# Two layers of an audio tower: the first feed-forward's residual in two VectorE steps, its second-norm statistics kept for all sequences, VectorE's loop written out

## The chip, the cores and the metric

The kernel runs on one core of a Trainium2 chip. The metric is the device time of one execution in microseconds (us), median of the runs. Engines are called PE (TensorE, matrix products), DVE (VectorE), ACT (ScalarE), POOL (GpSimd) and SP (which issues DMAs). Each engine takes its instructions in program order and waits on semaphores for the others.

## What is computed

Sixteen sequences of 256 tokens and 192 features pass a token selection (179 of 256 kept), and then two layers of attention and feed-forward, each ahead of a layer norm and with a residual. The part that the change touches is the second half of the first layer and the norm behind it:

```python
def _fq(x, scale, qmin, qmax):
    q = jnp.clip(jnp.round(x / scale), qmin, qmax) * scale
    return x + jax.lax.stop_gradient(q - x)
...
h = jnp.einsum('bsd,hd->bsh', x, _quant_weight(W1)) + b1
h = jax.nn.gelu(h, approximate=False)
h = _fq(h, s_gelu, -128.0, 127.0)
y = jnp.einsum('bsh,dh->bsd', h, _quant_weight(W2)) + b2
y = _fq(y, s_out, -128.0, 127.0)
...
h = h + _L0_ffn_ref(_layernorm(h, axis=-1), ...)
h = h + _L1_attn_ref(_layernorm(h, axis=-1), ...)
```

The second attention begins with a fake quantization whose scale is the largest absolute value of the whole normed tensor, over all 16 sequences. So nothing of the second attention can start before the last sequence has left the feed-forward and its norm.

## The kernel before

The residual stream of all sequences lies in SBUF (`resid`, 128 partitions, two token tiles of 128 and 51 rows per sequence). The program is written engine by engine, with semaphores; its stages follow one another. The change lies in the stage between the two attentions, the feed-forward of layer 0, which runs as a software pipeline over the 16 sequences (`ffn_step(i, par)` on PE, ACT and DVE).

- **PE**, step i: `ffn_turn(i)` transposes the normed sequence i + 1, `ffn_hidden(i)` makes the 768 hidden features of sequence i (24 f32 matmuls, L1909 and L1910), `ffn_out(i)` multiplies the quantized hidden features of sequence i - 1 with W2 (12 bf16 matmuls, L2078). `ffn_out(b)` waits for `hq_ready` (the quantized features from DVE) and for `f_added` of sequence b - 1, which frees its PSUM bank.
- **ACT**, step i: copies the transposed tile out of PSUM (L983), six Gelus (L994), one conversion to int32 (L1000), which sets `gelu_done`.
- **DVE**, step i, in this order: `ffn_norm` normalizes sequence i + 2 for the first norm (L1409); `ffn_add` takes y of sequence i - 2 out of PSUM and adds it to the residual in four dependent instructions, scale and bias (L1449), clip (L1453), round by adding and subtracting a large number (L1455), times `s_out` plus residual (L1458), through an f32 buffer `y_sb`; `hidden_round` clips the hidden features of sequence i - 1 to bf16 (L1465); `norm_max(i - 5)` normalizes sequence i - 5 for the second norm (L1488) and takes its largest absolute value (`top_abs`, L1497); `pair_tile_stats` takes mean and variance statistics of the newest residual (L1471, `bn_stats`).
- **POOL** first clears buffers for the next stages (memsets, L766 to L782), and then turns the statistics of two sequences at a time into mean and reciprocal standard deviation (`pair_norms`, L801 to L822: 20 links, each a tiny 128x4 instruction that waits for the one before). It waits for `pair_stats` ahead of them, and, ahead of L812, for `norm_used`.

The statistics and results for a pair stand in single buffers (`tstats`, `tmean`, `trstd`, four columns each). That is why POOL must wait at L812 until DVE has used the pair before, and DVE waits for `stats_taken` before it writes new statistics. DVE's steps 0 to 5 are written out, 6 to 13 are a hardware loop of two steps (`staged`), and the end is written by hand: the last two sequences get their statistics by DVE itself (`last_stats`, `last_pair`), and sequences 12 and 13 are normalized by POOL (L830).

When 14 sequences have their maximum, PE starts eight dummy products (`warm_up(8)`, L2041). Behind them it transposes the column of maxima (L2276, waits for `x_maxed`), then runs `warm_up(9)`, and then transposes the first quantized sequence for the second attention. DVE takes the overall maximum (L1567, then L1569 from PSUM) and quantizes (L1580 to L1586).

## Time and profile before

| | us |
|---|---|
| median of three runs (1355.39 to 1357.83) | 1355.62 |
| span of the profiled execution, first to last instruction | 1353.8 |
| outside the span, median less span | 1.8 |
| DVE, stage of the feed-forward: first `ffn_add` to the overall maximum | 842.7 to 941.5 |
| busy in the span: PE / DVE / ACT / POOL | 1116.0 / 1102.3 / 987.6 / 868.5 |

Times inside the profile are microseconds from the start of the span. In the timeline a row is one or more consecutive instructions of a kind: start, duration, engine, line, operation, output<-input and the count; the bracket tells how long the engine sat idle before it and what released it. POOLq stands for POOL's sequencer (a semaphore step without arithmetic). A row's duration overlaps the next row's start by the pipeline's length, so the cost of an instruction in a chain is the distance from start to start. In the table of windows each engine has its busy time with the number of instructions; PEclk is the granted clock of PE as a share of 2.4 GHz.

### The profile page before, as it was taken

To read this page: it belongs to the slowest core of one execution; us is meant where nothing else is said; L and a number is where in the kernel's file an instruction comes from. 1 tells how busy PE (TensorE), PEld (TensorE's weight loads), DVE (VectorE), ACT (ScalarE), POOL (GpSimd) and SP (SyncE) were. 2 spreads that over 40 slices of the span, in tenths; PEclk is the share of its full clock that TensorE was granted. 3 is DMA by queue.
4 is the path that set the end of the run, shared out by engine and by line. 5 is a ranking of instruction groups with operands and counts; after the bars stand their busy time and mean duration, and the time that the engine had idled before them with its cause. 6 is when DMAs were issued, how large, how long until landed. Compare 5 with 4: busy or idle time off the path is not lost. (4 is left out here: it accounts for less than half of the span.)

```text
span 1353.8 us, 40911 instructions
## 1 busy us (share of the span) xinstructions
PE 1116.0 (82%) x17093; PEld 855.6 (63%) x17093; DVE 1102.3 (81%) x2146; ACT 987.6 (73%) x921; POOL 868.5 (64%) x954
## 2 busy tenths in 40 slices
PE   3766877888787778788887877985999999998796
PEld 2454655666565556556665656883677777776595
DVE  7879989899999999999999994877567777777343
ACT  0469999999999999999999995772434444443232
POOL 4079889898889888988898897744011322324254
PEclk9889999999999999999999999997999999999698
DMA  9999999300000000000000001100000200002351
GB/s 251 360 361 359 355 339 335 102 11 11 10 8 5 11 10 2 10 11 10 2 11 10 11 2 48 24 0 0 2 2 2 65 19 18 16 12 56 108 153 56
DMA packets 78532, 107.61 MB, mean 79 GB/s; under 512 B 6963, under 2 KB 76489, under 8 KB 78356
## 3 DMA queue, kind: packets, MB, share of 16 engines
q1 hardware_dynamic: 66138, 90.93, 20.6%
q0 software_dynamic: 5360, 8.02, 1.8%
q10 hardware_dynamic: 6860, 6.12, 1.8%
q8 instruction: 135, 2.21, 0.7%
q14 instruction: 39, 0.32, 0.1%
HBM read 18.32 MB, written 83.85 MB: 75 GB/s over the span
## 5 line engine op out<-in xcount | busy, mean ns | idle before, releaser
L968 ACT ACTIVATE work<-work 128x2864 f32<-128x2864 f32 (+1 forms) x272 | 704.8, 2704 | 15.7 <-DVE work L446 14.8
L446 POOL TENSOR_TENSOR work<-shared 128x1253 f32<-128x1253 f32 (+1 forms) x272 | 613.1, 2268 | 114.3 <-PE psum L1956 78.8
L1956 PE MATMUL psum<-work,ws_place 128*32 128x179 f32 x8640 | 397.5, 322 | 148.6 <-ACT work L968 137.6
L446 DVE TENSOR_TENSOR work<-psum,shared 128x1611 f32<-128x1611 f32 (+3 forms) x288 | 488.0, 1723 | 0.5
L1956 PEld LDWEIGHTS psum<-work,ws_place 128*32 128x32 f32 x8640 | 264.3, 111 | 248.9 <-ACT work L968 191.4
L2154 PE MATMUL psum<-shared 32*64 32x179 f32 (+1 forms) x1728 | 129.4, 341 | 1.3 <-DVE peaks L1606 1.0
L957 ACT ACTIVATE pt_region<-psum,bs_neg 128x384 f32<-128x384 f32 x144 | 100.2, 697 | 2.9 <-PE psum L1968 2.9
L2154 PEld LDWEIGHTS psum<-shared 32*64 32x64 f32 (+1 forms) x1728 | 75.2, 147 | 40.5 <-issue 25.1
L1327 DVE SCALAR_TENSOR_TENSOR p_sb<-psum,bs_col,s_top 128x358 f32<-128x358 f32 x144 | 82.1, 570 | 14.9
L853 POOL DMA_INDIRECT xs_dram<-w_store,slot_i x24 | 26.6, 1107 | 93.2 <-DVE slot_i L1706 86.5
L801 POOL TENSOR_TENSOR tsum<-tstats 128x4 f32<-128x4 f32 x14 | 3.9, 279 | 116.7 <-DVE tstats L1471 116.2
L1324 DVE TENSOR_REDUCE s_top<-psum 128x2 f32<-128x358 f32 x144 | 71.7, 498 | 8.6 <-PE psum L1956 7.6
L1968 PE MATMUL psum<-ident,p_sb 128*128 128x128 f32 x416 | 78.1, 296 | 0.0
L1038 ACT ACTIVATE pt_region<-psum 128x1074 int32<-128x1074 f32 x48 | 51.2, 1067 | 33.0 <-PE psum L2154 33.0
L1045 ACT ACTIVATE pt_region<-psum 128x358 f32<-128x358 f32 x16 | 7.5, 469 | 87.6 <-PE psum L2203 87.6
L1628 DVE TENSOR_SCALAR pt_region<-pt_region 128x1074 uint32<-128x1074 uint32 x48 | 36.2, 755 | 42.5 <-ACT pt_region L1038 42.5
L1968 PEld LDWEIGHTS psum<-ident,p_sb 128*128 128x128 f32 x416 | 43.6, 142 | 41.3 <-issue 36.5
L881 POOL DMA_INDIRECT out<-shared x38 | 37.4, 985 | 42.7 <-DVE shared L1854 40.6
L1606 DVE TENSOR_REDUCE peaks<-psum 128x6 f32<-128x1074 f32 x48 | 59.9, 1273 | 4.2 <-PE psum L2154 4.1
L994 ACT ACTIVATE pt_region<-psum,b_col,w_scale 128x179 f32<-128x179 f32 x96 | 42.9, 497 | 19.1 <-PE psum L1910 19.1
L1847 DVE COPY shared<-psum 128x256 f32<-128x256 f32 x38 | 16.1, 425 | 48.6 <-PE psum L2353 48.5
L2123 PE MATMUL psum<-xqT,w1p 128*128 128x179 bf16 x480 | 45.2, 242 | 0.2 <-ACT xqT L1020 0.2
(406 smaller groups left out, 2029.2 us busy)
## 6 DMA issues: line engine op xcount, KB each, us to landing
xs_dram<-pad_row SPq DMA_DIRECT2D x23, 3088.0 KB, 27.8
pt_region<-xs_dram ACTq DMA_DIRECT2D x19, 193.0 KB, 2.6
pt_region<-xs_dram SPq DMA_DIRECT2D x19, 193.0 KB, 2.4
xs_dram<-pad_row SPq DMA_DIRECT2D x1, 2895.0 KB, 28.0
pt_region<-v_sb SPq DMA_DIRECT2D x22, 96.0 KB
work<-in_x SPq DMA_DIRECT2D x2, 768.0 KB, 10.2
work<-in_x ACTq DMA_DIRECT2D x2, 768.0 KB, 16.5
work<-in_L_ffn_W2T SPq DMA_DIRECT2D x1, 1536.0 KB
```

The source lines that it names most:

```text
L446: ins = eng.tensor_tensor(dst[:, a * KEEP:e * KEEP].rearrange("p (u s) -> p u s", s=KEEP), k[:, h * KP:h * KP + KEEP].unsqueeze(1).to_broa ...
L957: act.activation(pt[b % 2][:, 0:w + 1, k, :], bank_pt[p % 2][:, 0:128 * (w + 1)].rearrange("p (s c) -> p s c", c=128), ACT.Exp, bias=bs_ne ...
L968: act.activation(a, a, ACT.Tanh).then_inc(tanh_done, 1)
L994: ins = act.activation(gelu[par][:, c * KEEP:(c + 1) * KEEP], ffn_banks[par][c // 2][:, c % 2 * KEEP:(c % 2 + 1) * KEEP], ACT.Gelu, bias=b ...
L1038: act.activation(pt1[b % 2][:, r, :, :].rearrange("p (k s) t -> p k s t", s=2).bitcast(I32), score_slots[(r + 1) % 2], ACT.Copy).then_inc( ...
L1324: dve.tensor_reduce(top, s, AX.X, ALU.max).then_inc(top_step, 1)
L1327: dve.scalar_tensor_tensor(p_sb[p % 2][:, 0:w * ROW].rearrange("p (a s) -> p a s", s=ROW)[:, :, 0:KEEP], s, bs_col[:, :], top.unsqueeze(2) ...
L1606: dve.tensor_reduce(peaks[:, r, :].rearrange("p (s k c) -> p k s c", s=2, k=4)[:, 0:3, :, HD], score_slots[r % 2], AX.X, ALU.max, negate=T ...
L1956: ins = pe.matmul(bank_s[p % 2][32 * quad:32 * quad + 32, at:at + KEEP], ws_place[:, j, :], arg_slot(n)[:, u * KEEP:(u + 1) * KEEP], start ...
L1968: ins = pe.transpose(bank[:, 128 * s:128 * s + 128], src[:, 128 * s:128 * s + 128], ident[:, :])
L2123: ins = pe.matmul(out, lhs, rhs, start=(n == 0), stop=(n == len(terms) - 1))
L2154: return pe.matmul(out, one[32 * j:32 * j + 32, r, lo:hi], two[32 * j:32 * j + 32, r, 0:KEEP], start=True, stop=True)
```

## The change

The diff has five parts.

- **Residual in two steps.** `y_sb` becomes `y_int`, an int8 buffer. L1449 writes int8 directly; the clip and the rounding instructions are gone; the last instruction reads the int8. PE's `ffn_out(b)` waits for `y_step` (the first of the two) and not for `f_added`.
- **Statistics kept.** For the second norm DVE writes into the big arrays `stats`, `mean`, `rstd` (36 columns) of the first norm, at each sequence's own columns. `again_norms` on POOL replaces `pair_norms(j, 0)`, with the same 20 links and without the wait for `norm_used`; DVE no longer waits for `stats_taken` in this stage.
- **Order within DVE's step.** The statistics of sequence i - 2 are taken right after `hidden_round`, ahead of the second norm of sequence i - 5.
- **Loops written out.** DVE's steps 0 to 15 are all plain code, as are POOL's seven pairs.
- **The end of the stage.** DVE normalizes sequences 12 and 13 itself, in the gaps of `last_pair` between dependent tiny instructions; POOL's four instructions (L830) are gone. The last two sequences are normalized together and then reduced together.

```diff
-        y_sb = shared[:, 3584:3584 + 2 * D]
+        y_int = shared[:, 3584:3584 + D // 2].bitcast(I8).rearrange("p (t d) -> p t d", t=2)
...
-            with pool.Fori(0, B // 2 - 1) as j:
-                pair_norms(j, 0)
-            for b in (B - 4, B - 3):
-                for t, rows in TILES:
-                    k = 2 * (b % 2) + t
-                    ins = pool.tensor_scalar(xn3[0:rows, 2 * b + t, :], resid[0:rows, b + 1, t, :], tmean[0:rows, k:k + 1],
-                                             trstd[0:rows, k:k + 1], ALU.subtract, ALU.mult)
-                ins.then_inc(norm_used, 1)
+            def again_norms(j):
...
+                cols = slice(4 * j + 2, 4 * j + 6)
...
+                m, d, v, h, g, y = (a[:, cols] for a in (mean, diff, var, std, newt, rstd))
+                pool.wait_ge(pair_stats, 2 * j + 2)
...
+            for j in range(B // 2 - 1):
+                again_norms(j)
...
                 if real(i - 1):
-                    hidden_round(i - 1, 1 - par)
+                    hidden_round(i - 1)
                 if real(i - 2):
-                    dve.wait_ge(f_added, i - 1)
-                    need(dve, stats_taken, i - 2 - par)
+                    again_stats(i - 2)
                 if real(i - 5):
-                    norm_max(i - 5, 1 - par)
-                if real(i - 2):
-                    pair_tile_stats(i - 1, par)
+                    norm_again(i - 5)
+                    top_abs(i - 5)
...
-                dve.scalar_tensor_tensor(y.rearrange("p (t d) -> p t d", t=2), bank[:, 0:2 * D].rearrange("p (t d) -> p t d", t=2),
+                dve.scalar_tensor_tensor(y_int, bank[:, 0:2 * D].rearrange("p (t d) -> p t d", t=2),
                                          y_scale[:, :], b2_row[:, :].unsqueeze(1).to_broadcast([128, 2, D]),
                                          ALU.mult, ALU.add).then_inc(y_step, 1)
-                dve.wait_ge(y_step, n + 1)
-                dve.tensor_scalar(y, y, -128.0, 127.0, ALU.max, ALU.min).then_inc(y_step, 1)
-                dve.wait_ge(y_step, n + 2)
-                dve.tensor_scalar(y, y, MAGIC, MAGIC, ALU.add, ALU.subtract).then_inc(y_step, 1)
-                dve.wait_ge(y_step, n + 3)
-                r = resid[:, b + 1, :, :].rearrange("p t d -> p (t d)")
-                dve.scalar_tensor_tensor(r, y, s_out[:, :], r, ALU.mult, ALU.add).then_inc(f_added, 1)
+                dve.wait_ge(y_step, b + 1)
+                r = resid[:, b + 1, :, :]
+                dve.scalar_tensor_tensor(r, y_int, s_out[:, :], r, ALU.mult, ALU.add).then_inc(f_added, 1)
...
                 if b < B - 2:
                     dve.wait_ge(pair_norm, b - b % 2 + 2)
...
-            staged(dve, ffn_step, (2, 5), closed=True)
...
+            for i in range(B):
+                ffn_step(i)
+            norm_again(B - 5)
+            top_abs(B - 5)
             ffn_add(B - 2)
-            last_stats(0)
-            norm_max(B - 5, 1)
+            hidden_round(B - 1)
+            last_stats(B - 2)
             ffn_add(B - 1)
-            last_stats(1)
+            last_stats(B - 1)
             last_pair()
-            for b in range(B - 4, B):
-                norm_max(b, b % 2)
+            for b in (B - 2, B - 1):
+                norm_again(b)
+            for b in (B - 2, B - 1):
+                top_abs(b)
...
-                        pe.wait_ge(f_added, b)
+                        pe.wait_ge(y_step, b)
```

First place: DVE, one step in the middle of the stage, from `ffn_add` on. Before, in the loop; `work` is the normed sequence, `mx` its maxima, `pt_region` the hidden features:

```order
L1449 SCALAR_TENSOR_TENSOR shared<-psum,y_scale,b_row 128x384
L1452 ISA
L1453 TENSOR_SCALAR shared<-shared 128x384
L1454 REGISTER_ALU
L1455 TENSOR_SCALAR shared<-shared 128x384
L1456 REGISTER_ALU
L1458 ISA
L1458 SCALAR_TENSOR_TENSOR resid<-shared,s_out,resid 128x384
L1465 TENSOR_SCALAR pt_region<-pt_region 128x6x179
```

and with the change, the same place and what follows it in the step:

```order
L1476 SCALAR_TENSOR_TENSOR shared<-psum,y_scale,b_row 128x384
L1481 SCALAR_TENSOR_TENSOR resid<-shared,s_out,resid 128x384
L1487 TENSOR_SCALAR pt_region<-pt_region 128x6x179
L1227 BN_STATS stats<-resid 128x6
L1227 BN_STATS stats<-resid 51x6
L1509 TENSOR_SCALAR work<-resid,mean,rstd 128x192
L1509 TENSOR_SCALAR work<-resid,mean,rstd 51x192
L1516 TENSOR_REDUCE mx<-work 128x2
```

Two instructions and the register arithmetic of the loop are gone, and the statistics stand ahead of the second norm, where before they stood behind it.

Second place: DVE, the end of the stage. Before, after the last statistics, the first instructions of `last_pair`:

```order
L1526 TENSOR_TENSOR mean<-stats 128x4
L1527 TENSOR_TENSOR diff<-stats 128x4
L1528 TENSOR_TENSOR var<-stats 128x4
L1529 TENSOR_SCALAR mean<-mean 128x4
L1530 TENSOR_SCALAR var<-var 128x4
L1531 SCALAR_TENSOR_TENSOR diff<-diff 128x4
L1532 TENSOR_TENSOR var<-var,diff 128x4
L1533 TENSOR_SCALAR std<-var 128x4
L1534 CAST newt<-var 128x4
```

and with the change:

```order
L1546 TENSOR_TENSOR var<-stats 128x4
L1509 TENSOR_SCALAR work<-resid,mean,rstd 128x192
L1509 TENSOR_SCALAR work<-resid,mean,rstd 51x192
L1549 TENSOR_SCALAR mean<-mean 128x4
L1550 TENSOR_SCALAR var<-var 128x4
L1551 SCALAR_TENSOR_TENSOR diff<-diff 128x4
L1516 TENSOR_REDUCE mx<-work 128x2
L1554 TENSOR_TENSOR var<-var,diff 128x4
L1509 TENSOR_SCALAR work<-resid,mean,rstd 128x192
L1509 TENSOR_SCALAR work<-resid,mean,rstd 51x192
L1557 TENSOR_SCALAR std<-var 128x4
L1558 CAST newt<-var 128x4
```

The norm and maximum of sequences 12 and 13 have moved in between the tiny instructions; before, POOL did the norms and DVE took the maxima behind `last_pair`.

## Rows read from the trace of the kernel before

**Rows 1.** Table of windows: stretch, its length, busy time by engine, PE's clock
```profile
876.50:888.40 11.90, 10.37 (x83) 10.03 (x82) 9.59 (x25) 8.60 (x17) 5.94 (x26) 1.00 0.00 0
...
939.20:946.00 6.80, 6.80 (x23) 2.81 (x24) 5.06 (x18) 0.00 (x0) 0.00 (x0) 0.59 0.00 0
...
960.00:1200.00 240.00, 237.12 (x3139) 179.58 (x3137) 170.71 (x468) 106.81 (x205) 52.54 (x187) 1.00 0.06 18
```

**Rows 2.** Timeline of DVE in the loop: start, duration, what, idle before
```profile
876.52 0.66 DVE L1488 TENSOR_SCALAR work<-resid,tmean,trstd  x2 [1.57 <-POOLq L823]
...
877.79 0.60 DVE L1471 BATCH_NORM_STATS2 tstats<-resid 128x6 f32 x2
878.32 0.65 DVE L1409 TENSOR_SCALAR norm_wide<-resid,mean,rstd 128x192 f32 x2
878.88 0.60 DVE L1449 SCALAR_TENSOR_TENSOR shared<-psum,y_scale,b_row 128x384 f32<-128x384 f32 x1
...
888.39 0.66 DVE L1488 TENSOR_SCALAR work<-resid,tmean,trstd  x2 [1.58 <-POOLq L823]
```

**Rows 3.** Timeline of DVE in plain code behind the loop
```profile
913.91 0.59 DVE L1449 SCALAR_TENSOR_TENSOR shared<-psum,y_scale,b_row 128x384 f32<-128x384 f32 x1
914.53 0.36 DVE L1453 TENSOR_SCALAR shared<-shared 128x384 f32<-128x384 f32 x1
...
915.35 0.62 DVE L1458 SCALAR_TENSOR_TENSOR resid<-shared,s_out,resid 128x384 f32<-128x384 f32 x1
915.88 0.72 DVE L1465 TENSOR_SCALAR pt_region<-pt_region 128x1074 bf16<-128x1074 int32 x1
916.52 0.60 DVE L1471 BATCH_NORM_STATS2 tstats<-resid 128x6 f32<-128x192 f32 x2
917.05 0.64 DVE L1488 TENSOR_SCALAR work<-resid,tmean,trstd 128x192 f32<-128x192 f32 x2
...
918.19 0.61 DVE L1449 SCALAR_TENSOR_TENSOR shared<-psum,y_scale,b_row 128x384 f32<-128x384 f32 x1
```

**Rows 4.** Timeline of PE: the product with W2, once a step
```profile
858.63 1.15 PE L2078 MATMUL psum<-w2q,pt_region 128*128 128x192 bf16 x12
...
863.72 1.15 PE L2078 MATMUL psum<-w2q,pt_region 128*128 128x192 bf16 x12
...
869.93 1.16 PE L2078 MATMUL psum<-w2q,pt_region 128*128 128x192 bf16 x12 [0.97 <-DVE pt_region L1465]
```

**Rows 5.** Timeline of ACT: the conversion that sets gelu_done
```profile
864.85 1.19 ACT L1000 ACTIVATE pt_region<-pt_region,inv_gelu 128x1074 int32<-128x1074 f32 x1
```

**Rows 6.** Timeline of POOL: a memset, first and last arithmetic of pair 0
```profile
844.33 2.66 POOL L766 MEMSET work<- 128x3072 f32 x1 [0.15 <-POOL rstd L712]
...
856.35 0.40 POOL L801 TENSOR_TENSOR tsum<-tstats 128x4 f32<-128x4 f32 x1
...
864.31 0.20 POOL L822 TENSOR_TENSOR trstd<-trstd,tsum 128x4 f32<-128x4 f32 x1
```

**Rows 7.** Timeline of DVE beside those rows of POOL
```profile
844.68 2.88 DVE L1465 TENSOR_SCALAR pt_region<-pt_region 128x1074 bf16<-128x1074 int32 x1
...
864.76 0.66 DVE L1488 TENSOR_SCALAR work<-resid,tmean,trstd 128x192 f32<-128x192 f32 x2 [2.24 <-POOLq L823]
```

**Rows 8.** Timeline of DVE at the end of the stage
```profile
931.30 0.61 DVE L1518 BATCH_NORM_STATS2 stats<-resid 128x6 f32<-128x192 f32 x2
...
935.22 0.16 DVE L1540 SCALAR_TENSOR_TENSOR rstd<-above,rstd 128x4 f32<-128x4 f32 x1
...
938.48 0.55 DVE L1497 TENSOR_REDUCE mx<-work 128x2 f32<-128x384 f32 x1 [1.35 <-POOL work L830]
...
941.46 0.19 DVE L1567 TENSOR_REDUCE x_max<-mx 128x1 f32<-128x32 f32 x1
943.01 0.29 DVE L1569 TENSOR_REDUCE x_allmax<-psum 128x1 f32<-128x128 f32 x1 [1.36 <-PE psum L2276]
```

**Rows 9.** Timeline of PE there: the dummy products
```profile
939.18 3.57 PE L2041 MATMUL psum<-w2q,ident 128*128 128x512 bf16 x8 [12.56 <-DVE mx L1497]
```

127 lines of the change are left out of this document (71 added, 56 removed).

## The prediction

> **What bounds the kernel now.** I read the table of windows first. Behind the stage of the feed-forward, from 960 to 1200 us, PE is busy 237.12 of 240 us [rows 1]: what the feed-forward gives back there arrives as an earlier start of work that PE paces, and nothing in it hangs on an absolute time, so a shift passes through to the end. Within the stage, the window of one loop round (two steps) has PE busy 10.37 of 11.90 us and DVE 9.59 [rows 1]: neither is full. So the timeline. DVE's second norm comes at 876.52 and again, two steps later, at 888.39, both times after 1.57 or 1.58 us idle, released by POOL's sequencer [rows 2]. The round lasts 11.87 us; without the idle time DVE would need 10.29, that is 5.15 us a step. PE, where DVE is on time, comes back to the product with W2 after 863.72 - 858.63 = 5.09 us [rows 4]. So three clocks lie close together: POOL's chain over a pair (5.93 us a step as things stand), DVE's own work (5.15) and PE (5.09). The order of waits says which ends last: POOL, then DVE, then PE. PE's wait of 0.97 us for the hidden features [rows 4] is DVE being late.
>
> **Part 1, residual in two steps.** In plain code DVE's step from one L1449 to the next lasts 918.19 - 913.91 = 4.28 us, without an `ffn_norm` [rows 3]. The clip and the rounding take 915.35 - 914.53 = 0.82 us of it. `ffn_norm` adds 878.88 - 878.32 = 0.56 us [rows 2]. New step: 4.28 - 0.82 + 0.56 = 4.02 us, against PE's 5.09. The trace shows no int8. The nearest rows: L1465 converts int32 to bf16 in the same instruction that clips, 1074 elements in 0.72 us, so a conversion alone does not set a slower pace [rows 3]. I take 0 for it. The other end: each of the two instructions by 0.4 us slower (two thirds on top of 0.59 and 0.62). Below 0 nothing is likely, since both keep their 384 elements and their f32 operand. Even at 0.8 a step DVE would need 4.82 us, under 5.09; the 0.8 shows only where DVE is on the path: once at the start, and in the last steps. PE's earlier release (`y_step` for `f_added`) costs nothing and gives nothing, as PE is not held by the bank: its wait is for DVE's L1465.
>
> **Part 2, statistics kept.** POOL's links stay, only the wait at L812 goes. Undivided, the chain is seen at pair 0: 856.35 to 864.31 + 0.20, 8.16 us, and DVE starts 0.25 us later, at 864.76 [rows 6, 7]. New loop: the statistics that complete a pair are taken in step 2j + 3, the first norm that needs it stands right behind the statistics of step 2j + 5. That is two steps, 10.18 us at PE's pace, less about 0.5 for the statistics themselves (916.52 to 917.05 [rows 3]) but plus the same 0.5 two steps later. Needed: 0.1 + 8.16 + 0.25 = 8.5. Slack 1.7 us, so the wait of 1.58 us a round is gone and PE is late nowhere in the middle. What is late next is PE itself, 5.09 a step.
>
> **The start.** POOL clears buffers until 856.35, whatever DVE does, so pair 0 is ready for DVE at 864.76 as before [rows 6, 7]. DVE now arrives there some 4 us early and waits. From there to the hidden features of sequence 5: norm and maximum 918.19 - 917.05 = 1.14, `ffn_norm` 0.56, first residual step 0.62, second 915.88 - 915.35 = 0.53, then L1465 0.72 [rows 2, 3]. Sum 3.57: ready at 868.33, and PE starts the product 0.05 later, 868.38, where it started at 869.93 [rows 4]. Gain so far 1.55 us. The waits at memsets lie ahead of this point. First the row: L1465 at 844.68 lasts 2.88 us instead of 0.72, beside a memset of 2.66 us from 844.33 [rows 6, 7]. With the change, the first norm of sequence 5 or the next L1465 would sit behind a memset instead. It may cost PE 0.5 us, which the later wait for pair 0 swallows: I book 0.
> The Trainium skill (SBUF — State Buffer, the section on the two sides of its ports) says that VectorE in a 2-port mode and GpSimd take a shared port pair as an exclusive lock for a whole instruction; the trace agrees with the 2.88 us. By that rule the two instructions removed from each step (one source, SBUF to SBUF, 0.36 us for L1453) also stop holding up POOL's links, up to 4 x 0.36 = 1.4 us a pair; the chain would be 6.8 us and the sum below 1340.6. I keep 8.16, the measured one; this is case C.
>
> **The middle.** From 868.38, PE-paced: product of sequence 13 at 868.38 + 8 x 5.09 = 909.10. At the old pace it would be 869.93 + 4 x 11.87 = 917.4 [rows 2, 4]: the main gain, 8.3 us with the 1.55.
>
> **The end.** Gelus and conversion of a sequence end 864.85 + 1.19 - 863.72 = 2.32 us after PE starts the product of the sequence before [rows 4, 5]. So `gelu_done` of sequence 14 is at 911.4, L1465 ends at 912.15, the statistics of sequence 13 at 912.7. POOL: 912.75 + 8.16 = 920.9; DVE can normalize sequence 12 at 921.15. Does DVE get there in time? PE's product of sequence 15 needs its Gelus: product of 14 at 914.2, +2.32 +0.72, so 917.2; it lasts 1.15, and DVE adds 1.15 (0.62 + 0.53) and 0.1, then 0.61 for the last statistics: 920.3, plus the first three tiny instructions 0.3: 920.6. So `last_pair` waits about 0.5 us for POOL: a new wait, small, in place of the two for L830. Behind it: the tiny instructions, before 935.22 + 0.16 - (931.30 + 0.65) = 3.43 us [rows 8], less 0.35 already done, is 3.1; in between two norms and two maxima, 2 x 1.14 = 2.28, of which four gaps of about 0.1 between dependent instructions come back: 1.9. Then norms and maxima of 14 and 15, 2.28, and 0.1. Sum 7.4: the overall maximum at 921.15 + 7.4 = 928.5, before 941.46 [rows 8]. **Gain 12.9 us.** The two waits for POOL's L830 (the second, 1.35 us, at 938.48 [rows 8]) are part of it.
>
> **Behind the maximum.** Now L1567 to L1569 takes 943.01 - 941.46 = 1.55 us, with 1.36 idle, because PE is still in `warm_up(8)`, 939.18 + 3.57 = 942.75 [rows 8, 9]. With the change the dummies are released by the maximum of sequence 13, which stands some 4.5 us ahead of L1567 (two thirds of the tiny instructions' 3.1, and 2.4), so they end about 1 us before it; about 0.7 of the 1.55 goes. `warm_up(9)` then starts 0.7 earlier relative to the maximum, and the first transposition of the second attention stands behind it. I take **0.7**. What it hangs on is PE's clock: granted 0.59 over 939.2 to 946.0 [rows 1], that is 1.2 GHz for most of it, after PE had idled 12.56 us. The change puts a gap of 1 us into that stretch. If the clock rises right with `warm_up(9)`, 9 products take half of 4 us and the gain is 1.4; if it rises later than before, `warm_up(9)` takes 9 x 3.57 / 8 = 4.0 and the next products run slow too: -1.0.
>
> **Sum.** 12.9 + 0.7 = 13.6 us off the span of 1353.8: 1340.2, and with the 1.8 us outside the span 1342.0.
>
> **Rivals.**
> *A, POOL's chain is longer than its slack.* Unwaited it runs beside a denser DVE. In the middle it decides from 10.2 us a pair; at the end every us counts at once. For: DVE rows show that one engine can hold the other for a whole instruction [rows 6, 7]. Against: 8.16 already includes such delays. A chain of 10 us gives 1342.0 + 1.8 = 1343.8, one of 11 gives 2.8 at the end and 0.8 x 6 rounds: 1349.6.
> *B, int8 is slow*, 0.8 us a step: 868.38 moves by 0.8, and at the end 0.8 more of the two last additions passes POOL's time: 1343.6.
> *C, a shorter chain.* It is 1 us shorter without the removed instructions beside it, and the clock returns early (0.7): 1340.3; with pair 0 also 1 us earlier, 1339.3.
> *D, the kept statistics don't free DVE*: POOL's links still begin only behind a norm. Then a round is POOL's chain plus one DVE step, and only that step's 0.82 counts: 6 x 0.82 = 4.9 in the middle, at the end 1.6 for the last two additions and about 1.8 for the L830 that is gone, 8.3 in all: 1347.3. Against: the waits for `norm_used` and `stats_taken` that tie them are struck.
> *E, slower than before: the clock.* If PE stays at 1.2 GHz after the new gap, the second attention, where PE is busy 237.12 of 240 us [rows 1], loses half of each us. It decides from 27 us of such running, which would eat the 13.6. For: the clock was at 0.59 there. Against: it came back within 6.8 us of dense work [rows 1], and that work stays.
> Writing out the loops by itself I book at 0: at the loop's head L1409 starts 878.32 - 877.79 = 0.53 us behind the statistics, and in plain code the next instruction comes after the same 0.53 [rows 2, 3]. Nor do I expect a loss from the longer program.
>
> **How the numbers follow.** Forecast 0.74; A 0.09, B 0.05, C 0.07, D 0.03, E 0.02. A measurement tells 0.2%, 2.7 us, from no change. The forecast's own spread is 1340 to 1344. The range takes in C and the milder A and B: 1339.0 to 1346.0. Faster 0.97 (all but E and a little), same 0.01, slower 0.02.
>
> **What would show it.** In the changed profile: products with W2 5.09 us apart without idle time from sequence 6 on (right), or waits for DVE (part 1 or 2 wrong); no POOL release of a second norm in the middle, one at the start at about 864.8 of some 4 us, one of about half a us in `last_pair`; L1476 and L1481 at 0.6 us each (B wrong); L1567 near 928.5; PE's clock at 1.00 when the second attention's first products run. A wait of DVE for POOL in every round would make the prediction wrong, towards A or D.

## The result, and the profile after

The changed kernel takes 1339.3 us, the median of four runs (1338.75 to 1339.52); the kernel before, run beside it, 1356.5 (1355.39 to 1357.83). The ratio is 0.987, 95% interval 0.9856 to 0.9884. It is faster by 17.2 us, where 13.6 had been forecast; 1342.0 against the 1355.62 of before would have been 0.990, and the low end of the range, 1339.0, is 0.9877. Direction and mechanism came as forecast, the size did not. Two runs of 2134 and 3612 us, far above all others (1333 to 1366 us), are left out of every ratio below.

The profiled executions have spans of 1353.8 and 1337.4 us. I cut both into stages, each between two instructions of DVE that both kernels have (us; the starts and ends are read from rows like those below):

| stage | before | after | difference |
|---|---|---|---|
| start to first `ffn_norm` (code unchanged) | 820.6 | 820.8 | +0.2 |
| first `ffn_norm` to the overall maximum | 120.9 | 106.3 | -14.6 |
| maximum to the first attention shift | 15.9 | 16.0 | +0.1 |
| first to last shift (second attention) | 274.5 | 274.5 | 0 |
| last shift to the routing's counts | 30.0 | 28.9 | -1.1 |
| counts to the first expert sequence | 14.6 | 13.4 | -1.2 |
| the rest | 77.4 | 77.6 | +0.2 |

DVE's waits in the stage, first before, then after from 865 us on (who waited for what: us in total, times, longest):

```profile
DVE work L1488 <- POOLq L823: 10.7, 6, 2.2
DVE mx L1497 <- POOL work L830: 2.5, 2, 1.4
```

```profile
DVE shared L1476 <- PE psum L2097: 8.5, 8, 1.5
DVE work L1509 <- POOLq L859: 0.3, 1, 0.3
```

The first of the six waits for POOL's statistics before, 2.24 us for pair 0 at 864.76, has its counterpart after in the 3.12 us at 864.03 (shown below), which the second view leaves out. The five behind it [rows 2] are gone, and a new one of 0.28 us stands at the end. What DVE waits for in the middle is PE's product, that is, PE paces. PE's view of it after (timeline, the product with W2):

```profile
862.40 1.15 PE L2097 MATMUL psum<-w2q,pt_region 128*128 128x192 bf16 x12
867.79 1.16 PE L2097 MATMUL psum<-w2q,pt_region 128*128 128x192 bf16 x12 [0.15 <-DVE pt_region L1487]
872.89 1.15 PE L2097 MATMUL psum<-w2q,pt_region 128*128 128x192 bf16 x12
877.98 1.15 PE L2097 MATMUL psum<-w2q,pt_region 128*128 128x192 bf16 x12
...
903.41 1.15 PE L2097 MATMUL psum<-w2q,pt_region 128*128 128x192 bf16 x12
908.50 1.15 PE L2097 MATMUL psum<-w2q,pt_region 128*128 128x192 bf16 x12
```

The product at 867.79 is that of sequence 5, the one at 908.50 that of sequence 13; before, they stood at 869.93 [rows 4] and at

```profile
916.66 1.16 PE L2078 MATMUL psum<-w2q,pt_region 128*128 128x192 bf16 x12 [0.78 <-DVE pt_region L1465]
```

From 867.79 to 908.50 the products are 5.08 to 5.10 us apart with no wait, as [rows 4] had it for a single step. The table of windows says the same: over the stretch that [rows 1] show for before (10.37 of 11.90 us), PE now is busy all the time, and it is so over two steps of 10.17 us:

```profile
876.50:888.40 11.90, 11.90 (x95) 11.73 (x94) 9.85 (x26) 9.54 (x20) 7.90 (x36) 1.00 0.00 0
...
886.00:896.17 10.17, 10.17 (x82) 10.06 (x81) 8.16 (x21) 8.45 (x17) 5.78 (x27) 1.00 0.00 0
```

The start, on DVE (timeline), the rows that answer to [rows 7]:

```profile
864.03 0.73 DVE L1509 TENSOR_SCALAR work<-resid,mean,rstd 128x192 f32<-128x192 f32 x2 [3.12 <-POOLq L859]
...
865.85 0.60 DVE L1476 SCALAR_TENSOR_TENSOR shared<-psum,y_scale,b_row 128x384 int8<-128x384 f32 x1
866.48 0.62 DVE L1481 SCALAR_TENSOR_TENSOR resid<-shared,s_out,resid 128x384 f32<-128x384 int8 x1
867.02 0.72 DVE L1487 TENSOR_SCALAR pt_region<-pt_region 128x1074 bf16<-128x1074 int32 x1
```

and on POOL, its first and last arithmetic of pair 0, against [rows 6]:

```profile
856.60 0.27 POOL L839 TENSOR_TENSOR mean<-stats 128x4 f32<-128x4 f32 x1
...
863.75 0.20 POOL L858 TENSOR_TENSOR rstd<-rstd,newt 128x4 f32<-128x4 f32 x1
```

The end, on DVE, against [rows 8]:

```profile
920.15 0.66 DVE L1509 TENSOR_SCALAR work<-resid,mean,rstd 128x192 f32<-128x192 f32 x2 [0.28 <-POOLq L859]
...
927.10 0.19 DVE L1591 TENSOR_REDUCE x_max<-mx 128x1 f32<-128x32 f32 x1
927.86 0.29 DVE L1593 TENSOR_REDUCE x_allmax<-psum 128x1 f32<-128x128 f32 x1 [0.57 <-PE psum L2295]
```

Int8 costs nothing: L1476 and L1481 start 0.63 and 0.54 us before their successors, as with f32 [rows 3]. The overall maximum has moved from 941.46 to 927.10.

These rows cut the stage into three parts, and all that follows is easier to read with them. In us, from the first `ffn_norm` to the product of sequence 5, from there to the product of sequence 13, and from there to the overall maximum:

| kernel | start | middle | end | stage |
|---|---|---|---|---|
| before | 49.34 | 46.73 | 24.80 | 120.9 |
| run 1 below, the two-step residual alone | 47.61 | 42.60 | 23.49 | 113.7 |
| run 2 below, the rest of the change alone | 48.96 | 40.70 | 20.57 | 110.2 |
| after | 46.99 | 40.71 | 18.60 | 106.3 |

Two more profiles of the kernel before (that of run 4, and run 10) have 49.7, 46.7 or 46.8, and 24.8, two more of the changed one 46.7 to 46.9, 40.7 and 18.6. So the end gained as much, 6.2 us, as the middle, 6.0.

### The profile page after: what moved, and what is told of

It is laid out like the page before. It is cut to its first block and busy times, and to the rows that moved or that the text cites. A ratio compares the mean times of both kernels' runs of the same rounds, so it can differ in the third digit from the quotient of the medians.

```text
span 1337.4 us, 40560 instructions
## 1 busy us (share of the span) xinstructions
PE 1112.1 (83%) x17090; PEld 853.0 (64%) x17093; DVE 1095.7 (82%) x2118; ACT 986.9 (74%) x921; POOL 864.4 (65%) x950
## 3 DMA queue, kind: packets, MB, share of 16 engines
q1 hardware_dynamic: 66138, 90.93, 20.8%
## 5 line engine op out<-in xcount | busy, mean ns | idle before, releaser
L801 POOL TENSOR_TENSOR tsum<-tstats 128x4 f32<-128x4 f32 x7 | 1.9, 275 | 108.5 <-DVE tstats L1498 108.5
L1024 ACT ACTIVATE pt_region<-psum,b_col,w_scale 128x179 f32<-128x179 f32 x96 | 42.9, 497 | 15.8 <-PE psum L1929 15.8
## 6 DMA issues: line engine op xcount, KB each, us to landing
work<-in_x ACTq DMA_DIRECT2D x2, 768.0 KB, 16.2
```

Of the source, the lines that this page charges most:

```text
L1024: ins = act.activation(gelu[par][:, c * KEEP:(c + 1) * KEEP], ffn_banks[par][c // 2][:, c % 2 * KEEP:(c % 2 + 1) * KEEP], ACT.Gelu, bias=b ...
```

## The experiments

Stage times below are from the profile of each run: "the stage" is from the first `ffn_norm` to the overall maximum (before 120.9, after 106.3). Medians of the kernel before, run beside the experiments, were 1356.4 to 1356.8.

**1. The two-step residual alone**, on the kernel before:

```diff
-        y_sb = shared[:, 3584:3584 + 2 * D]
+        y_int = shared[:, 3584:3584 + D // 2].bitcast(I8).rearrange("p (t d) -> p t d", t=2)
...
-                dve.tensor_scalar(y, y, -128.0, 127.0, ALU.max, ALU.min).then_inc(y_step, 1)
...
-                dve.tensor_scalar(y, y, MAGIC, MAGIC, ALU.add, ALU.subtract).then_inc(y_step, 1)
```

> The kernel before with the two-step residual alone (int8 buffer, clip and rounding instructions gone, pair buffers and loops as before). Theory P (a round of two steps is POOL's chain plus one DVE step): only one step's 0.8 to 1.0 us counts in each of the four waited rounds, 3.6 us, and about 2.4 at start and end: 6 us less than before, rounds of 11.0 us, DVE's wait for POOL grows from 1.6 to about 2.4. Rival W (DVE's work is what paces the round): twice that in each round, 9.6 us less, rounds of 10.1.

Measured: 1347.6 us, ratio 0.9937 (0.9921 to 0.9952), the stage 113.7. DVE's waits for POOL in the loop (timeline):

```profile
886.13 0.66 DVE L1482 TENSOR_SCALAR work<-resid,tmean,trstd  x2 [2.15 <-POOLq L823]
896.94 0.66 DVE L1482 TENSOR_SCALAR work<-resid,tmean,trstd  x2 [2.15 <-POOLq L823]
```

A round is 10.81 us, not 11.87, and the wait for POOL in it has grown from 1.58 to 2.15. With a wait for POOL in every round, the round cannot be PE's 10.17. It is POOL's chain plus one step of DVE, since POOL may begin its second half only when DVE has used the pair before. The rows give the two terms of the 1.06 us: from one second norm of DVE to the next in the same round it is 4.29 us and not 5.14 (0.85 less, where I had counted 0.82 a step), and from POOL's L812 to the norm that it releases 5.71 and not 5.92 (0.21 less). The second step's saving goes into the wait. The median, 9.0 us under the kernel before, is nearer to what rival W had (9.6) than to theory P (6); it is the rounds and the grown wait that speak for P, and P's sum left out too much at the start and the end.

**2. The statistics, the order and the end alone**, that is the changed kernel with the four-instruction residual put back:

```diff
-                dve.scalar_tensor_tensor(y_int, bank[:, 0:2 * D].rearrange("p (t d) -> p t d", t=2),
+                dve.scalar_tensor_tensor(y.rearrange("p (t d) -> p t d", t=2), bank[:, 0:2 * D].rearrange("p (t d) -> p t d", t=2),
...
+                dve.tensor_scalar(y, y, -128.0, 127.0, ALU.max, ALU.min).then_inc(y_step, 1)
...
+                dve.tensor_scalar(y, y, MAGIC, MAGIC, ALU.add, ALU.subtract).then_inc(y_step, 1)
```

> The changed kernel with the four-step residual of before (f32 buffer, clip, rounding) put back, everything else as changed. Theory P (PE paces the middle at 5.09 us, DVE with 4.84 stays under it): products with W2 stay 5.09 apart, and only the start (0.6) and the end (about 1.6) lose: 2 to 3 us slower than the changed kernel, 1341.5 to 1342.5. Rival W (the two halves of the change add up to DVE's time saved): 13 x 0.4 or more, over 5 us slower, 1344.5 or more.

Measured: 1345.3 us, ratio 0.9921 (0.9904 to 0.9938), the stage 110.2. The products with W2:

```profile
868.45 1.17 PE L2103 MATMUL psum<-w2q,pt_region 128*128 128x192 bf16 x12 [0.23 <-DVE pt_region L1493]
873.55 1.15 PE L2103 MATMUL psum<-w2q,pt_region 128*128 128x192 bf16 x12
...
904.07 1.15 PE L2103 MATMUL psum<-w2q,pt_region 128*128 128x192 bf16 x12
909.15 1.15 PE L2103 MATMUL psum<-w2q,pt_region 128*128 128x192 bf16 x12
```

In the middle they are 5.09 apart, as in the changed kernel. So the middle does not need the two-step residual: the kept statistics give it, together with the new order in DVE's step and the loops written out. Run 3 takes the loops out of that; the order was not tried by itself. The 3.9 us of the stage that are missing lie at its ends: the product of sequence 5 stands 868.45 - 819.49 = 48.96 us behind the first `ffn_norm`, with the whole change 867.79 - 820.80 = 46.99; from the product of 13 to the maximum it is 929.72 - 909.15 = 20.57 against 927.10 - 908.50 = 18.60. On top of the rest, the two-step residual gives 2.0 us at the start and 2.0 at the end, and nothing in between. The two halves alone save 7.2 and 10.7 us of the stage, together 14.6: they share 3.3.

The median is 6.0 us over the changed kernel's, and by that number alone rival W (over 5) would be right and theory P (2 to 3) wrong. The products 5.09 apart rule W out as the mechanism. P missed 1 to 2 us in the stage, and the rest lies far behind it: last shift to counts took 30.0 us in this profile and counts to experts 14.8, where the changed kernel had 28.9 and 13.4.

**3. The loops written out alone**, on the kernel before:

```diff
-            staged(dve, ffn_step, (2, 5), closed=True)
+            for i in range(B - 2):
+                ffn_step(i, i % 2)
```

> The kernel before with DVE's and POOL's loops written out and nothing else. The prediction booked 0. Theory L (register instructions in the loop body cost DVE time: a step is 5.15 us in the loop, 4.85 in plain code with the norm added): with POOL's chain in the round one step's 0.3 counts, 4 x 0.3 = 1.2 us less than before. Rival 0: no difference.

Measured: 1356.7 us, ratio 1.0 (0.9983 to 1.0017). The rounds are 11.76 us (waits for POOL at 884.00, 895.75, 907.51), and the wait in them is 1.90 and not 1.58: what DVE saves in plain code it waits more for POOL. The 0 that I had booked stands for the median. The profiled execution is an odd one (1349.9 us, the fastest of the ten), with a stage of 122.7 us: the first product with W2 came 22.5 us behind the first `ffn_norm`, where all but one of the other profiles have 20.8 to 20.9, and the next had to wait 3.19 us for L1465, which took 3.00 us instead of 0.72 beside a memset. So the start in a single profile can be off by 1 to 3 us.

**4. PE's clock at the routing.** PE's dummy products now fill the time in which it idles there, in the kernel before and in the changed one:

```diff
             prefix_mm(B - 3)
+            warm_up(10)
             prefix_mm(B - 2)
...
+            warm_up(24)
             for n in range(RING):
                 pe.wait_ge(sent[n], 32 * B // RING)
-            warm_up(8)
+            warm_up(14)
```

> The kernel before with more dummy products on PE in its last part: 10 ahead of the last but one count of experts' tokens, 24 ahead of the wait for the sent rows, 14 instead of 8 behind it. Theory C (2.1 us of the gain arose there, because the return of PE's clock to 2.4 GHz fell differently into the same work): both kernels with this edit lose most of their time at 1.2 GHz there, this one is 1 to 3 us faster than before, and the difference to the changed kernel with the same edit is 14.3 us. Rival: the edit does nothing to the difference, it stays 16.4.

> The changed kernel with the same dummy products. Theory C: 14.3 us under the other with this edit, 0 to 1.5 us faster than the changed kernel. Rival: 16.4 us under it.

Measured: 1354.6 us (ratio 0.9985, 0.9974 to 0.9996) and 1340.2 us (0.9877, 0.9861 to 0.9894). The medians differ by 14.5 us. Last shift to counts and counts to experts took 28.4 and 13.4 us on the kernel before (30.0 and 14.6 without the edit), and 28.7 and 13.2 on the changed one (28.9 and 13.4). So the edit takes 2.8 us out of these two parts of the kernel before and 0.4 out of those of the changed one: with PE's clock mostly kept up, the 2.3 us that set the two kernels apart there are gone. The difference of the medians, 14.5, is near that of the feed-forward stages (121.2 and 106.0, so 15.2), and does not have the 16.4 of the spans above.

**5. A delay ahead of the maximum**, on the changed kernel, with 7 and with 14 tiny dependent memsets:

```diff
+            for n in range(7):
+                rlink(dve.memset(slot_f[:, :], 0.0))
             dve.wait_ge(qv_blank, 4)
```

> The changed kernel with 7 tiny dependent memsets on DVE ahead of the overall maximum, 1.4 us of delay. Theory C (phase of PE's clock): the stretch from the last part on changes its own length by up to 1 or 2 us either way against the changed kernel. Rival: everything behind is shifted by 1.4 us, its length unchanged within 0.2.

> The same with 14 memsets, 2.8 us. Theory C: the length of the last part differs from that with 7 or 0 memsets by several tenths of a us or more, with other stretches at 1.2 GHz. Rival: shifted by 2.8 us, same length.

Measured: 1339.3 us (two runs, 1336.95 and 1341.58) and 1342.2 us (1341.27 and 1343.02). The memsets took 0.12 us each, not 0.2: the delay was 0.8 and 1.7 us. Last shift to counts was 29.1 and 29.9. It would be wrong to read the 0.8 us between them as the price of the longer delay. The stages are 108.0 and 107.8 us: in the first profile PE's first product came 22.5 us behind the first `ffn_norm` (run 3 has the other such case) and the product of sequence 5 0.95 us later than in the changed kernel, in code that the edit leaves as it is. So both reached their last shift at nearly the same moment, 1220.0 and 1220.3 us, and yet took 29.1 and 29.9 us from there. What these runs show is that an unchanged part 275 us behind an edit can come out 1 us longer; not that the delay decides it. With two runs each the medians say nothing.

**6. POOL normalizes 12 and 13 again**, on the changed kernel, with the last four maxima taken together:

```diff
             for j in range(B // 2 - 1):
                 again_norms(j)
+            pool.wait_ge(norm_used, B - 2)
+            for b in (B - 4, B - 3):
+                for t, rows in TILES:
...
-                norm_again(B - 4)
-                top_abs(B - 4)
...
-            pe.wait_ge(n3_step, B - 2)
-            warm_up(8)
+            pe.wait_ge(pair_norm, B - 2)
+            warm_up(13)
```

> The changed kernel, but POOL normalizes sequences 12 and 13 behind its last pair, as it did before the change; DVE takes the maxima of 12 to 15 together behind its own two norms. PE's dummy products ahead of the maximum are released by POOL's last pair, 13 in place of 8. What it prices: the part of the change that gave these two norms to DVE. In the changed kernel POOL's last pair is ready at 919.9 and one POOL norm instruction took 1.00 us before, so POOL is done at 924.2; DVE saves two norms and the 0.28 wait, is through last_pair at 923.2, with the norms of 14 and 15 at 924.4, and four maxima of 0.47 end at 926.3: overall maximum 0.8 us earlier than the changed kernel's (relative to its first ffn_norm 105.5 in place of 106.3). If the given-over norms are what the end gained from, as my sum had it (two norms and maxima fitted into gaps), it is 1 to 2 us later instead (107.3 to 108.3), because POOL's norms are stretched by DVE's instructions beside them.

Measured: 1338.6 us (1333.86 to 1340.78), the stage 105.9: 0.4 less, not 0.8, and not more. POOL's four norms ran 4.09 us from 920.33, and all four maxima stood behind their end:

```profile
924.85 1.93 DVE L1523 TENSOR_REDUCE mx<-work 128x2 f32<-128x384 f32 x4
926.89 0.19 DVE L1594 TENSOR_REDUCE x_max<-mx 128x1 f32<-128x32 f32 x1
```

That DVE normalizes these sequences itself is therefore not what the end gained from. What is gone in both is a wait of POOL's last chain for DVE, in the middle of its links; I take it for the main part of the end's gain, but no run removes it alone. In the kernel before (POOL's timeline):

```profile
928.85 0.20 POOL L812 TENSOR_TENSOR tmean<-tsum,tnum 128x4 f32<-128x4 f32 x1 [2.48 <-DVE work L1488]
```

The run changed a second thing, the dummy products, which POOL's last pair now releases. PE idled 3.14 us ahead of them and not 5.78, and the nine dummies behind the maximum ran at full speed:

```profile
927.29 2.11 PE L2063 MATMUL psum<-w2q,ident 128*128 128x512 bf16 x9
```

From the maximum to the first shift it is 14.4 us and not 16.0, as in run 7 below. Of these 1.6 us the routing took most back: last shift to counts is 30.3 us.

**7. PE kept on ahead of the maximum**, on the changed kernel:

```diff
+            pe.wait_ge(y_step, B - 1)
+            warm_up(26)
             pe.wait_ge(f_added, B)
             pe.wait_ge(n3_step, B - 2)
-            warm_up(8)
+            warm_up(14)
```

> The changed kernel with 26 more dummy products on PE behind its last product with W2 and 14 in place of 8 ahead of the maximum, so that PE does not idle for 5.8 us there. Clock theory: the granted clock stays at 1.00 through the maximum, the 9 dummies behind it last 2.0 instead of 4.0 us, the first quantized sequence is turned when DVE has it (2.9 us behind the maximum, now 4.3), and DVE's first instruction on the second attention's values comes 7.4 to 7.6 us behind the maximum instead of 8.92: 1.3 to 1.5 us less, so about 1338 where the changed kernel has 1339.3. Rival: the clock falls or returns by something else than PE's idle time there, the 9 dummies stay at 4.0 us and nothing changes (under 0.3 us).

Measured: 1339.7 us (1337.21 to 1339.9). The dummies behind the maximum, changed kernel first, then this one (PE's timeline):

```profile
923.27 3.19 PE L2060 MATMUL psum<-w2q,ident 128*128 128x512 bf16 x7 [5.78 <-DVE mx L1516]
927.35 0.48 PE L2295 MATMUL psum<-ident,x_max 128*128 128x128 f32 x1 [0.88 <-DVE x_max L1591]
927.62 3.99 PE L2060 MATMUL psum<-w2q,ident 128*128 128x512 bf16 x9
```

```profile
918.81 8.58 PE L2060 MATMUL psum<-w2q,ident 128*128 128x512 bf16 x39
928.60 0.32 PE L2297 MATMUL psum<-ident,x_max 128*128 128x128 f32 x1 [1.21 <-DVE x_max L1591]
928.76 2.11 PE L2060 MATMUL psum<-w2q,ident 128*128 128x512 bf16 x9
```

The clock theory holds: nine dummies take 2.11 and not 3.99 us, and DVE's first instruction on the second attention's values comes 935.67 - 928.36 = 7.31 us behind the maximum, not 936.02 - 927.10 = 8.92. From the maximum to the first shift it is 14.4 us and not 16.0. From the first `ffn_norm` to the end only 0.8 us of it was left (515.8 against 516.6), and nothing in the median: last shift to counts, unchanged code, came out at 30.0 and not 28.9. The windows of the same 12 us there, 18 us behind the last shift, changed kernel and this one (PEclk is the third number from the right):

```profile
1235.50:1247.50 12.00, 5.61 (x41) 3.49 (x41) 9.00 (x62) 2.30 (x3) 6.60 (x8) 0.77 0.21 69
```

```profile
1235.20:1247.20 12.00, 7.03 (x41) 4.34 (x41) 8.31 (x57) 2.30 (x3) 6.38 (x7) 0.56 0.21 68
```

PE is busy 5.61 us for 41 products at a mean clock of 0.77, and 7.03 us for as many at 0.56.

**8. A shorter chain**, on the changed kernel: two refinements of the reciprocal root in place of three for pairs 0 to 6, 16 links in place of 20.

```diff
-                for n in range(3):
+                for n in range(2):
```

> The changed kernel with two refinements of the reciprocal root in place of three in POOL's chain for pairs 0 to 6 (16 links, not 20; it leaves a refinement out). Prices the chain. Four links at 0.28 are 1.1 us. Theory: the start hangs on POOL's last memset plus the chain, so pair 0 is ready 1.1 us earlier, PE's product with W2 of sequence 5 comes 1.1 us earlier (966.7 less 100: at 866.7 in place of 867.8), the middle is PE's (5.09 apart) and keeps it, and at the end the wait of 0.28 for POOL goes: overall maximum 1.1 to 1.4 us earlier relative to the first ffn_norm (104.9 to 105.2 in place of 106.3). Rival: at the start DVE or PE is next within 0.3 us and the gain stops there: 105.7 to 106.3.

Measured: 1339.6 us (1338.16 to 1340.0), the stage 105.4, 0.9 less: between the two expectations. (The "966.7 less 100" in the expectation is a slip; 866.7 is meant.) PE's product of sequence 5 now starts at 867.55, which is 5.08 behind the one before, without a wait: 46.45 us behind the first `ffn_norm`, 0.54 earlier than in the changed kernel. The other half of the 1.1 us is stopped by PE. So in the changed kernel POOL's chain at the start is within 0.6 us of no longer mattering.

**9. All that lowered a part, together** (the edits of 6 and 4, and 26 and 14 dummies as in 7), and the changed kernel once more, beside it on the same chip:

> The changed kernel with all that lowered a part of its profile: POOL normalizes 12 and 13, PE's dummy products fill the time ahead of the maximum (26 and 14) and the idle time of the routing (10, 24, 14). By the parts of the single profiles: first ffn_norm to maximum 105.9 (106.3), maximum to first shift 14.3 (16.0), last shift to counts 28.5 (28.9) with PE's clock at 1.00 throughout, counts to the experts 13.2 (13.4): 2.6 us off the profiled span, and off the median against the changed kernel run beside it, 1336.5 to 1337.5. If the clock's gains ahead of the second attention are given back at the routing, as with the kept-on PE alone (30.0 there), although PE is filled there too, the last shift to counts is again near 30 and the whole is within 1.5 us of the changed kernel.

> The changed kernel once more, unaltered, with more rounds. What it settles: how much of the 3.6 us by which the gain exceeded the forecast is the kernel's and how much is the spread of the runs. By the stage of the feed-forward alone (14.6 us less, of which the forecast had 12.9) and nothing elsewhere the ratio is 0.9892; with 1.1 us more at the routing (clock back in time) 0.9884; the first measurement had 0.987. Its profile tells, too, whether last shift to counts stays at 28.9 or comes out at 30.0 in another execution of the same program, and how far the first ffn_norm moves from 820.8.

Measured: 1337.7 us (1336.6 to 1338.67; ratio 0.986, 0.9845 to 0.9876) and 1341.5 us (1339.49 to 1344.02; 0.9896, 0.9881 to 0.9911). Beside each other the intervals don't meet: the combination is faster than the changed kernel, by 3.7 us of median here, by 2.0 us in the profiles from the first `ffn_norm` to the end (514.9 and 516.9). The changed kernel's 1341.5 is its highest median, though; against its other two (1339.3 above, 1339.7 in run 10) the gain is 1.6 to 2.0 us, and their intervals do meet this one. The 2.0 of the profiles is the better figure. Maximum to first shift came out at 14.4 as expected. At the routing the gain did not come, last shift to counts 29.0. PE's clock fell there, where the same dummies on the changed kernel (run 4) had kept it. Windows of 12 us of run 4 and of this one, and one of 9 us of this one:

```profile
1234.80:1246.80 12.00, 9.38 (x65) 4.94 (x65) 9.44 (x63) 2.30 (x3) 6.81 (x8) 1.00 0.21 68
```

```profile
1234.90:1246.90 12.00, 9.21 (x58) 4.62 (x58) 9.46 (x62) 2.30 (x3) 6.50 (x8) 0.85 0.20 67
...
1240.90:1249.90 9.00, 7.69 (x33) 3.34 (x32) 5.04 (x30) 1.77 (x2) 5.86 (x6) 0.63 0.25 85
```

In the 6 us in which the fall begins (from 1237.90 here, from 1237.80 in run 4), PE was busy 3.79 us here and 3.65 there, so the busy time does not tell the two apart. The second profile of the changed kernel has the same parts as the first: stage 106.2, last shift to counts 28.8, counts to experts 13.4.

**10. Both kernels again**, on one chip, unaltered, to tell the program from chance:

> The kernel before, unaltered, profiled once more. If the clock's course at the routing belongs to the program: last shift to counts 30.0 again and counts to the experts 14.6, span about 1354 and ratio 1.0. If it is chance: 28.5 to 29.0 and 13.4, with a span near 1351.5. First ffn_norm between 814 and 822 either way.

> The changed kernel, unaltered, a third time, beside the kernel before on one chip. By its parts: first ffn_norm to maximum 106.2 or 106.3, last shift to counts 28.8 or 28.9, counts to experts 13.4 if these belong to the program. Ratio between the two measured so far, 0.987 and 0.9896; forecast 1342.0 / 1355.6 was 0.990.

Measured: 1356.4 us (ratio 1.0007, 0.9987 to 1.0027) and 1339.7 us (0.9875, 0.9848 to 0.9902). The kernel before has the stage at 121.3, last shift to counts 30.0 again, but counts to experts 13.5 and not 14.6. The changed kernel has 106.0, 29.2 and 13.1. The windows at the routing, before, before again, and the third profile of the changed kernel:

```profile
1249.80:1261.80 12.00, 7.26 (x42) 4.34 (x41) 8.30 (x57) 2.30 (x3) 6.36 (x7) 0.59 0.20 67
```

```profile
1251.20:1263.20 12.00, 7.01 (x40) 4.33 (x41) 8.30 (x57) 2.30 (x3) 6.35 (x7) 0.58 0.20 68
```

```profile
1237.50:1249.50 12.00, 5.51 (x40) 3.39 (x40) 9.00 (x60) 2.30 (x3) 6.32 (x7) 0.78 0.20 67
```

So of the 2.3 us at the routing, some 1 us (30.0 to about 28.9) comes back in each profile of the two programs, and the other 1.2 does not: that was chance in the one profile of before.

## Why the forecast was right and where it was wrong

**Which step failed.** The order of the bounds was right; the sizes in the sum were not. With the parts of the profiles (forecast, then measured): start of the stage 1.55 and 2.35 us, middle 6.0 and 6.0, end 5.4 and 6.2 (the forecast's products and maximum against the old kernel's rows), behind the maximum 0.7 and -0.1, routing nothing and 2.3, all other parts nothing and -0.4. Together 13.6 and 16.4 us of the span. The forecast failed at three terms, then: POOL's chain, kept at 8.16 us, which measured 7.35 at the start and 7.87 at the end; the clock behind the maximum; and the routing, which was put at nothing because a shift "passes through to the end".

**The bound and the middle: right.** POOL's waits are gone, PE paces at 5.09 us a step, a new wait of 0.28 us for POOL stands in `last_pair` (0.5 forecast). Runs 1 and 2 show which part did it. A step of DVE without waits takes 4.05 us (L1476 at 865.85 and 869.90), where the sum had 4.02. Case D is out, and so is the idea that DVE's own work was the bound: the residual alone left the wait for POOL in each round.

**POOL's chain: the term that was too long.** I booked 8.16 us with the sentence "I keep 8.16, the measured one". After, pair 0 took 863.95 - 856.60 = 7.35, and DVE was released at 864.03 where 864.76 was forecast: 0.08 us behind the chain's end and not 0.25 (it is 0.25 where POOL's pairs are a loop, before and in run 1, and 0.08 where they are written out, after and in run 2). Measured from the first `ffn_norm`, the product of sequence 5 gained 2.35 us and not 1.55: 0.8 more. At the end the same term returned 0.4: `last_pair`'s first norm came 920.15 - 908.50 = 11.65 us behind the product of sequence 13, and 12.05 was forecast.

The 8.16 was itself a chain stretched by DVE's instructions beside it. It is 8.16 to 8.20 us in all three profiles of the kernel before and in run 2, which keep the four-instruction residual and begin the chain behind the memsets, and 7.30 to 7.35 in nine of the ten profiles with the two-step residual and all 20 links, run 1 among them (7.65 in the tenth, run 5). So it is the residual's two instructions that make the difference there. The way is only half of it the one that case C names. Before, links of POOL and what DVE ran beside them:

```profile
856.86 0.55 POOL L803 TENSOR_TENSOR tvar<-tstats 128x4 f32<-128x4 f32 x1
...
857.58 0.45 POOL L805 TENSOR_TENSOR tvar<-tvar,tnum 128x4 f32<-128x4 f32 x1 [0.17 <-POOL tvar L803]
```

```profile
856.73 0.62 DVE L1458 SCALAR_TENSOR_TENSOR resid<-shared,s_out,resid 128x384 f32<-128x384 f32 x1
857.26 0.72 DVE L1465 TENSOR_SCALAR pt_region<-pt_region 128x1074 bf16<-128x1074 int32 x1
```

and after, the two links that are still stretched:

```profile
859.32 0.51 POOL L851 TENSOR_TENSOR newt<-newt,tnum 128x4 f32<-128x4 f32 x1
859.90 0.55 POOL L852 TENSOR_TENSOR std<-var,tnum 128x4 f32<-128x4 f32 x1
```

```profile
859.15 0.62 DVE L1481 SCALAR_TENSOR_TENSOR resid<-shared,s_out,resid 128x384 f32<-128x384 int8 x1
859.68 0.72 DVE L1487 TENSOR_SCALAR pt_region<-pt_region 128x1074 bf16<-128x1074 int32 x1
```

A link usually takes 0.20 us. Those beside the removed clip and rounding (L801 with 0.40, L820 with 0.27, L821 with 0.31) lost 0.4 us together. The larger stretches stand beside L1458 and L1465, which both kernels have: before, two such pairs fell into the chain, after only one, since DVE is earlier and has the first pair behind it when the chain begins. That is another 0.6 us, less 0.2 for a norm that now meets the chain's first links. Where the chain starts within DVE's step matters as much as what DVE runs: in run 3's profile the chain began elsewhere in the step and took 7.32 us with all four instructions. Case C had a shorter chain, at 1 us and with 0.07 of the chance; it deserved more, since a sign of the stretching stood in [rows 6]: the chain's first instruction with 0.40 us, its last with 0.20. The Trainium skill (SBUF — State Buffer, the section on the two sides of its ports) would have given an estimate of 6.8 us by its rule of the exclusive lock. By that rule, the direction agrees with the trace and the size does not: the 1.4 us of that estimate were 0.4.

**The end: 0.4 us too long.** From the first norm of `last_pair` to the maximum I had 7.4 us and the trace has 927.10 - 920.15 = 6.95. The links hidden under norms and maxima gave back more than the four gaps that I counted. (The 3.43 us of tiny instructions in that sum should read 3.47, as [rows 8] have the last statistics at 0.61 us and not 0.65; and the old kernel's product of sequence 13, reckoned as 917.4, stood at 916.66. Neither changes the forecast, which takes the maximum before from its row.) Together with the start this makes the stage's gain 14.6 and not 12.9 us (0.8 + 0.8, and 0.1 of rounding); further profiles have 121.3 against 106.2 and 106.0, 15.1 to 15.3.

**Behind the maximum: the clock's term failed.** I booked 0.7 us for dummies that end earlier. L1591 to L1593 did fall, from 1.55 to 0.76. But PE is held by its own clock: `warm_up(9)` took 3.99 us, so PE turned the first quantized sequence 4.3 us behind the maximum (931.44), where DVE had it ready at 2.8. The part is as long as it was, 16.0 against 15.9, and in the later profiles longer, 16.2 against 15.7. Run 7 shows that the clock is the reason: kept up, it makes the part 14.4. I had put the price of the clock between -1.0 and 1.4 and taken 0.7, above the middle of the two; the 4.0 us for nine dummies is just what I had written for the bad side.

**The routing: not in the sum at all.** I wrote that a shift "passes through to the end". Through the second attention it did, to 0.1 us. At the routing, where PE's clock falls and comes back, the same code took 28.8 to 29.2 us in three profiles of the changed kernel and 30.0 in both of before, so 1 us came on top; the other 1.2 us (counts to experts) were chance, by run 10. I had asked of the clock only whether it would stay low for 27 us (case E, which did not happen), and not whether a place with a falling clock further down would come out otherwise.

**Cases A and B** did not happen: no longer chain, no cost of int8.

**The base and the range.** 1355.62 was the median of three runs; the medians of 4 to 19 runs since lie at 1356.4 to 1356.8, so 0.8 to 1.2 us of the difference are the base. The three measurements of the change read 0.987, 0.9896 and 0.9875. The forecast of 0.990 is inside the interval of the second and third and outside that of the first. The first `ffn_norm`, at the end of a part that nothing touches, stood between 814.0 and 822.7 us in the profiles. The range had its lower end at the sum of all of case C; a spread of 2 us in base and medians, and of 1 to 2 us at the places where the clock falls, belonged on top of it. In us the three measurements are 17.2, 15.1 and 17.1; from the first `ffn_norm` to the end the first pair of profiles differs by 16.6 and the later ones by 15.5. What the medians have on top of that no profile here explains.

**What stays open.** Why the clock comes back earlier at the routing in some programs. Last shift to counts took 28.8 to 29.2 us in the changed kernel, with the two-step residual alone, with the shorter chain, with 7 memsets of delay and in the combination; it took 29.9 to 30.3 in both profiles of before, in runs 2 and 3, with 14 memsets, with PE kept on, and with POOL's norms. Counts to experts ranges from 13.0 to 15.8 (run 1). The first of the two repeats for a program and shifts with small edits 275 us ahead; the moment of arrival alone does not tell, since last shifts at 1217.2 (run 7) and 1217.2 (run 8) gave 30.0 and 29.2.

## What to carry to other kernels

When two engines hand single buffers to and fro, a round is the helper's chain plus one step of the other. Of the work removed from the other engine's two steps, only one step's share shortens the round; the other's lengthens its wait (run 1). Look at what lets the helper start. Take the length of a dependent chain from a place where the engine beside it is idle and from one where it is busy, and carry both. Where PE's clock falls and returns, expect 1 to 2 us of unchanged code to move with any shift, in either direction, and test it by filling PE there. Compare parts of the profile that repeat (here the middle and the end of the stage, within 0.1 us) before comparing medians that move by 1 to 2 us.

## What the runs showed of the hardware that I had not expected

- An int8 output from PSUM and an int8 input cost DVE nothing: 0.62 and 0.62 us for 384 elements, 0.60 and 0.62 with f32 throughout.
- A memset of POOL can hold more than one step of DVE: after the change L1439 took 3.32 us (two instructions, 0.65 usual) at 845.26 and L1487 2.48 (0.72) at 849.67, both beside memsets of 2.65 us, and PE waited only 0.17 us for it (the rows below). With the four-instruction residual (run 2) the second hold fell on the clip, 2.66 us at 848.28 for 0.36, and PE waited 2.12 us. Which instruction meets the memset decides whether such a hold costs something.
- Dummy products that keep PE's clock up in one program need not do so in another: 0.63 of full speed as the mean over 9 us in run 9, where the same dummies alone, on the changed kernel, kept it at 1.00 in every 3 us of the 50 us behind the last shift (run 4), with about the same busy time ahead of the place.
- A dependent 128x4 instruction takes POOL 0.28 us from start to start; beside some of DVE's it takes 0.5 to 0.7. On DVE such a link takes 0.20, and a tiny memset 0.12.

DVE, POOL and PE in the changed kernel (timelines), for the second point:

```profile
845.26 3.32 DVE L1439 TENSOR_SCALAR fnorm<-resid,mean,rstd 128x192 f32<-128x192 f32 x2
...
849.67 2.48 DVE L1487 TENSOR_SCALAR pt_region<-pt_region 128x1074 bf16<-128x1074 int32 x1
```

```profile
845.03 2.66 POOL L766 MEMSET work<- 128x3072 f32 x1 [0.15 <-POOL rstd L712]
...
848.93 2.65 POOL L771 MEMSET work<- 128x3072 f32 x1
```

```profile
852.22 1.16 PE L2097 MATMUL psum<-w2q,pt_region 128*128 128x192 bf16 x12 [0.17 <-DVE pt_region L1487]
```
